# A transformer block on one core: the first two batches and the last one reordered

## The reference

```
h = gelu(x[1:] @ W1 + x[0] @ W2 + b)                      # 255 tokens
q, k, v = layernorm(h) @ qkv_w.T                           # 16 heads of 64
a = softmax(q k.T / 8 + bias[rel_bucket]) v                # per head
h = h + a @ o_w.T
h = h + (silu(layernorm(h) @ wg.T) * (layernorm(h) @ wu.T)) @ wd.T   # int weights / 127
```

## Time and profile before

| | us |
|---|---|
| median of 3 runs | 1799.73 (1798.41 to 1800.47) |
| profiled execution | 1802.05 |
| span of its instructions | 1799.9 |

### The profile page before, as it was taken

How to read it: one execution, slowest core, us unless ns; L and a number is a source line. 1 busy time by engine, 2 the same in 40 slices (tenths; PEclk the granted TensorE clock), 3 DMA queues, 4 the chain that set the end, 5 groups by cost and what they waited for, 6 DMA issues and landing times.

```text
span 1799.9 us, 47320 instructions
## 1 busy us (share of the span) xinstructions
PE 1765.0 (98%) x17460; PEld 1649.0 (92%) x17460; DVE 1517.0 (84%) x4832; ACT 1391.5 (77%) x3784; POOL 1165.3 (65%) x1493
## 2 busy tenths in 40 slices
PE   8899999999999999999999999999999999999997
PEld 6789999999999999999999999999999999999996
DVE  6788888988888988888988888888888888889885
ACT  6777778777787787877877778777787777877873
POOL 2666656766656766666766567666567666667663
PEclk9999999999999999999999999999999999999998
DMA  6200000000000000000000000000000000000000
GB/s 197 60 7 16 17 16 4 14 16 16 17 16 5 14 16 16 16 10 10 13 16 16 16 8 10 16 16 17 16 5 13 16 16 16 16 5 13 7 7 13
DMA packets 26777, 34.13 MB, mean 19 GB/s; under 512 B 3457, under 2 KB 20402, under 8 KB 26546
## 3 DMA queue, kind: packets, MB, share of 16 engines
q1 hardware_dynamic: 26368, 30.95, 5.8%
q10 hardware_dynamic: 178, 0.13, 0.0%
HBM read 22.65 MB, written 8.42 MB: 17 GB/s over the span
## 4 chain that ended last, share of the span: by engine, by line
PE 95%; DVE 2%; POOL 1%; ACT 1%; issue 1%; DMA 0%; POOLq 0%; DVEq 0%; ACTq 0%
PE ps L484 56%; PE ps L569 14%; PE ps L545 13%; PE ps L558 7%; PE ps L493 3%; PE ps L513 2%; DVE prob L992 1%; DVE pT L1000 0%; DMA staged<-w_v 0%; POOL prob L420 0%; PE ps L507 0%; ACT prob L802 0%; POOL wo L397 0%; DVE wg L923 0%; ACT xt L769 0%
## 5 line engine op out<-in xcount | busy, mean ns | idle before, releaser
L420 POOL TENSOR_TENSOR prob<-prob,inv 128x510 f32<-128x510 f32 x512 | 524.0, 1037 | 369.5 <-DVE inv L1005 369.5
L809 ACT ACTIVATE pT<-ps 128x512 fp32r<-128x512 f32 x512 | 278.3, 596 | 326.9 <-PE ps L558 326.9
L802 ACT ACTIVATE prob<-prob,neg_top 128x255 f32<-128x255 f32 x1024 | 506.9, 502 | 4.8 <-DVE neg_top L992 4.4
L992 DVE CUSTOM_DVE_ANT_0 prob<-ps,bias 128x255 f32<-128x255 f32 x1024 | 380.2, 420 | 98.9 <-PE ps L545 92.0
L484 PE MATMUL ps<-xnT,wqk 128*128 128x256 f32 x3072 | 414.6, 284 | 1.4 <-DVE qk L970 1.4
L484 PEld LDWEIGHTS ps<-xnT,wqk 128*128 128x128 f32 x3072 | 379.4, 188 | 13.8 <-DVE qk L970 1.6
L1000 DVE TENSOR_TENSOR pT<-ps,pT 128x512 fp32r<-128x512 f32 x512 | 334.6, 685 | 1.5 <-ACT pT L809 1.5
L569 PE MATMUL ps<-pT,v 128*128 128x256 f32 x2048 | 297.1, 288 | 20.2 <-DVE pT L1000 10.6
L569 PEld LDWEIGHTS ps<-pT,v 128*128 128x128 f32 x2048 | 265.8, 191 | 37.5 <-issue 30.8
L545 PE MATMUL ps<-qk 64*128 64x256 f32 x3072 | 252.4, 297 | 0.0
L545 PEld LDWEIGHTS ps<-qk 64*128 64x128 f32 x3072 | 198.8, 186 | 35.0 <-issue 0.8
(11 more groups left out here) (94 smaller groups left out, 2587.4 us busy)
## 6 DMA issues: line engine op xcount, KB each, us to landing
xt<-x_cols SPq DMA_DIRECT2D x32, 256.0 KB, 2.7
out<-xt SPq DMA_DIRECT2D x32, 128.0 KB, 1.7
r_rows<-readout_rows SPq DMA_DIRECT2D x30, 128.0 KB, 2.9
out<-xt SPq DMA_DIRECT2D x32, 112.0 KB, 1.9
bias<-bias_rows SPq DMA_DIRECT2D x8, 384.0 KB, 5.2
staged<-w_qk SPq DMA_DIRECT2D x8, 256.0 KB, 5.2
staged<-w_v SPq DMA_DIRECT2D x4, 256.0 KB, 5.8
staged<-w_o SPq DMA_DIRECT2D x4, 256.0 KB, 5.8
```

The costliest lines, as they stand in the source:

```text
L420: pool.tensor_tensor(pr, pr, by, ALU.mult).then_inc(prob_done, 1)
L802: ex = act.activation(pr, pr, ACT.Exp, bias=neg_top[:, g % 2, hh, t:t + 1], scale=-1.0, accum_out=total[:, g % 2, hh, t:t + 1])
L809: act.activation(transposed(0, half), transposed_in(half), ACT.Copy).then_inc(pT_hi, 1)
L992: ins = dve.tensor_tensor_reduce(prob[:, g % 2, hh, t, 0:S], ps[:, bank_s[hh], t * T:t * T + S], falling(2 * g + hh, WINDOW - 1 - b0), 1.0 ...
```

## The change

It reorders the written-out pipeline at three places. The computation is the same; the only new instructions are matmuls of `keep_busy`.

1. **First steps.** In step 0 DVE and ACT do the bias of the second head, both exponentials and both inverses of pair 0 before the low and high parts of weight pieces 6 to 9. Pieces are spread differently over steps 0 to 3 (10 and 11 stay in step 1, 12 and 13 in step 2, 14 to 16 in step 3), POOL's low part of piece 14 moves one step later. ACT does its pieces ahead of `heads_moved`, and DVE its pieces ahead of `heads_added` and of the first head's `add_bias` in all steps with pieces (0 to 10).
2. **Values of batch 0 and 1.** `values(0, 1)` goes behind the transposes of step 1, `values(0, 2)` from step 2 to step 4, `values(0, 3)` from step 4 to step 5 and into `bank_f`. `norm_transposed(0, 1)` writes `bank_f` and no longer waits for `probs_lo` of pair 4. ACT and DVE take `values(1, 1)` at the end of step 9, not in step 10 behind the probabilities. Five `keep_busy` matmuls stand ahead of the value product in steps 2 and 7, written into `bank_a`.
3. **The end.** In step 256 the transposes of the last pair come ahead of the projection; `down(30)` is cut in two halves of three tiles, one in step 256 and one in step 257; DVE takes its result (`output(30)`) ahead of the last `residual`; `keep_busy` has 9 and 3 matmuls around the value product of step 256 and 17 ahead of the last `norm_transposed`.

The core of the diff (in order: tables and banks, TensorE, ACT, DVE; the calls of `ln_bank` and `v_bank` get the batch, and the old place of ACT's pieces at the end of `step` is removed):

```diff
-        PIECES_AT = {0: (6, 7, 8), 1: (9, 10, 11), 2: (12, 13, 14), 3: (15, 16), 4: (17, 18),
+        PIECES_AT = {0: (6, 7, 8, 9), 1: (10, 11), 2: (12, 13), 3: (14, 15, 16), 4: (17, 18),
                      5: (19, 20), 6: (21, 22), 7: (23, 24), 8: (25,), 9: (26,)}
...
-        def ln_bank(n):
-            return (bank_t[1], bank_f)[n]
-
-        def v_bank(n):
-            return bank_s[0] if n == 3 else bank_f
+        def ln_bank(n, batch):
+            return bank_f if n == 1 or batch == 1 else bank_t[1]
+
+        def v_bank(n, batch):
+            return bank_s[0] if n == 3 and batch > 0 else bank_f
...
-                def keep_busy(n):
+                def keep_busy(n, bank=bank_qk):
                     for _ in range(n):
-                        pe.matmul(ps[:, bank_qk, 0:P], ident[:], ident[:], start=True, stop=True)
+                        pe.matmul(ps[:, bank, 0:P], ident[:], ident[:], start=True, stop=True)
 
...
-                def down(batch, has_lo):
-                    for m in range(MT):
+                def down(batch, has_lo, tiles=range(MT)):
+                    for m in tiles:
...
-                    mm.then_inc(dn_mm, 1)
+                    if m == MT - 1:
+                        mm.then_inc(dn_mm, 1)
...
-                            pe.wait_ge(v_lo, count(4, i, 0))
-                            values(i, 1)
-                        if g == 2 and i >= 2:
-                            if i < B:
-                                pe.wait_ge(biased, count(H, i, 2))
-                            else:
-                                pe.wait_ge(biased, count(H, B - 1, H - 1))
+                            if i > 0:
+                                pe.wait_ge(v_lo, count(4, i, 0))
+                                values(i, 1)
+                        if g == 2 and 2 <= i < B:
+                            pe.wait_ge(biased, count(H, i, 2))
                             down(i - 2, has_lo)
-                        if g == 4 and i < B:
+                        if G in (4, 5):
+                            pe.wait_ge(v_lo, count(4, 0, G - 3))
+                            values(0, G - 2)
+                        if g == 4 and 0 < i < B:
                             pe.wait_ge(biased, count(H, i, 6))
                             values(i, 3)
...
-                            pe.wait_ge(pT_lo, count(H, i, 8))
+                            if i > 0:
+                                pe.wait_ge(pT_lo, count(H, i, 8))
+                            else:
+                                pe.wait_ge(v_lo, count(4, 0, 3))
...
+                        if G == 1:
+                            pe.wait_ge(v_lo, count(4, 0, 0))
+                            values(0, 1)
+                        if g == 2 and 0 < i < B:
                             pe.wait_ge(v_lo, count(4, i, 1))
...
-                    if i < B:
-                        early()
+                    early()
+                    if G == PAIRS * B:
+                        keep_busy(9)
                     if pair(G - 2):
                         if pair(G - 3):
                             pe.wait_ge(o_added, count(PAIRS, *pair(G - 3)))
+                        if G in (2, 7):
+                            keep_busy(5, bank_a)
                         values_probs(*pair(G - 2))
+                    if G == PAIRS * B:
+                        keep_busy(3)
+                        transpose_banks_free()
+                        probs_transposed(*pair(G - 1))
                     if pair(G - 3):
                         bb, gg = pair(G - 3)
                         if gg == 0 and bb > 0:
                             pe.wait_ge(h1_done, count(1, bb - 1))
                         project(bb, gg)
-                    if i == B:
-                        early()
+                    if G == PAIRS * B:
+                        pe.wait_ge(biased, count(H, B - 1, H - 1))
+                        down(B - 2, has_lo, range(0, MT // 2))
+                    if G == PAIRS * B + 1:
+                        down(B - 2, has_lo, range(MT // 2, MT))
                     if pair(G):
                         score_banks_free()
                         scores(i, g)
                     if G == 0:
                         queries_keys(0, 1)
-                    if pair(G - 1):
+                    if pair(G - 1) and i < B:
                         transpose_banks_free()
                         probs_transposed(*pair(G - 1))
                     late()
 
                 def finish(has_lo):
+                    keep_busy(17)
                     norm_transposed(1, B - 1)
...
-                    if g == 2 and i < B:
+                    if g == 2 and i < B and i != 1:
                         values_hi(i, 1)
                     if g == 7 and prev:
                         tanh(i - 1, 4)
-                    if pair(G - 1):
+                    if pair(G - 1) and G > 1:
                         exps(*pair(G - 1), 0)
...
-                    if g == 4 and i < B:
+                    if g == 4 and 0 < i < B:
                         values_hi(i, 3)
+                    if G in (4, 5):
+                        values_hi(0, G - 2)
...
+                    if G == 0:
+                        exps(0, 0, 0)
+                        exps(0, 0, 1)
                     if g == 0 and 0 < i < B:
                         values_hi(i, 0)
+                    if g == 1 and i == 1:
+                        values_hi(i, 1)
...
+                    for n in PIECES_AT.get(G, ()):
+                        if n < FIRST_INT:
+                            piece_high(n)
...
-                    if g in (5, 7) and pair(G - 2):
+                    if i > 0 and g in (5, 7) and pair(G - 2):
                         probs_lo(*pair(G - 2), 1)
-                    if pair(G - 1):
+                    if pair(G - 1) and G > 1:
                         add_bias(*pair(G - 1), 1)
-                    if g not in (5, 7) and pair(G - 2):
+                    if (i == 0 or g not in (5, 7)) and pair(G - 2):
                         probs_lo(*pair(G - 2), 1)
                     if pair(G - 2):
                         probs_lo(*pair(G - 2), 0)
...
-                    if g == 2 and 2 <= i < B:
+                    if g == 2 and i >= 2:
                         output(i - 2)
...
+                    if G == 0:
+                        add_bias(0, 0, 1)
+                        inverse(0, 0, 0)
+                        inverse(0, 0, 1)
                     if g == 0 and 0 < i < B:
                         values_lo(i, 0)
+                    if g == 1 and i == 1:
+                        values_lo(i, 1)
...
                     if g == 3 and i == B:
-                        output(B - 2)
                         normalise(1, B - 1)
...
-                    if g != 1 and pair(G - 2):
-                        heads_added(*pair(G - 2))
-                    if pair(G) and G > 0:
-                        add_bias(i, g, 0)
                     for n in PIECES_AT.get(G, ()):
                         if n < FIRST_INT and n not in POOL_PIECES:
                             piece_low(n)
                     for n in PIECES_AT.get(G - 1, ()):
                         if n >= FIRST_INT:
                             piece_low(n)
+                    if g != 1 and pair(G - 2):
+                        heads_added(*pair(G - 2))
+                    if pair(G) and G > 0:
+                        add_bias(i, g, 0)
```

More of the change, by code:

```diff
@@ L512, in norm_transposed @@
                         for t in range(TT):
-                            mm = pe.transpose(ps[:, ln_bank(n), k * T + t * P:k * T + (t + 1) * P],
+                            mm = pe.transpose(ps[:, ln_bank(n, batch), k * T + t * P:k * T + (t + 1) * P],
                                               normed[:, t, k * P:(k + 1) * P], ident[:])
@@ L532, in values @@
                         pe.wait_ge(piece_lo, V_ALL if n else V_FIRST)
-                    split_mm(ps[:, v_bank(n), :], lambda a, k: xnT[:, a, k, t * P:(t + 1) * P],
+                    split_mm(ps[:, v_bank(n, batch), :], lambda a, k: xnT[:, a, k, t * P:(t + 1) * P],
                              lambda b, k: wv[:, b, k, half * 512:(half + 1) * 512], range(KD)
@@ L658, in score_banks_free @@
                             pe.wait_ge(out_done, count(1, i - 2))
-                        if g == 4:
+                        if g == 4 and i > 0:
                             pe.wait_ge(v_lo, count(4, i, 3))
@@ L783, in norm_hi @@
                     dst = (xnT, hnT)[n]
-                    act.activation(dst[:, 0].rearrange("p k n -> p (k n)"), ps[:, ln_bank(n), :], ACT.Copy
+                    act.activation(dst[:, 0].rearrange("p k n -> p (k n)"), ps[:, ln_bank(n, batch), :], ACT.Copy
                                    ).then_inc(lnT_hi[n], 1)
@@ L794, in values_hi @@
                     dst = v[:, t, half * 4:half * 4 + 4, :].rearrange("p g (s d) -> p g s d", d=DH)
```

(13 more changed lines are left out.)

6 lines of the change are left out of this document (3 added, 3 removed).

## The result

The changed kernel takes 1796.1 us (median of 18 runs, 1794.49 to 1797.29); the kernel before, on the same chip in the same session, 1800.2 us (18 runs, 1797.09 to 1803.17). The ratio is 0.9978, 95% interval 0.9971 to 0.9985: 0.22% faster, 4.1 us of the 8.1 forecast, at the edge of the range. The profiled execution of the changed kernel took 1795.17 us, 3.37 of them outside its span of 1791.8 us.

A forecast was written before the change was run, and what follows sets the result against it. PE was taken as full from 100 to 1763 us, so only its idle time and lowered clock at both ends could gain: head 3.6 plus end 4.5, 8.1 us off 1799.7, giving 1791.6 us; range 1788.5 to 1796.2.

The forecast's parts named there:

- First product, step 2: First value product: 0.69 us later, at 35.6, perhaps 0.86 shorter if idle matmuls hold the clock; together nothing.
- a late landing of piece 11: Step 2: weight piece 11 might land at 33.3 instead of the assumed 31.0, 2.3 us too late.
- Steps 3 to 5: Moved values groups of batch 0: POOL sets the pace, projection again at 56.6 to 56.7, gain 0 plus or minus 1.
- Steps 6 to 10: Later head: products at 61.2, 69.7 and 91.4; the head gains 3.6 us at full clock, 2.5 at half.
- steps 6 to 8: Transposes off the wait (0.69) and pieces filling DVE's waits (1.3): product of pair 4 gains 2.0 us.
- The end: From 1763.7 us: last transposes at 1780.0, not 1784.49, gain 4.5 us; 17 idle matmuls overrun by 0.35.
- (c): Rival, chance 0.04: idle matmuls do not hold the clock at the end; slower, 1804.0 us.
- (a): Rival, chance 0.22: the end gains, but DVE pieces held up by POOL cost the head's 3.6 us; 1795.2 us.
- (b): Rival, chance 0.13: POOL gets ahead in steps 3 to 5, step 10's gap shrinks below 2 us; 1788.5 us.
- (d): Rival, chance 0.08: waits move to other engines at both ends, 1.5 us in each; 1797 us.
- Sum: Whole kernel: head 3.6 plus end 4.5 gives 8.1 us, taken from the median 1799.7 to 1791.6.
- its two cases: Step 10, gap of 2.4 us: head gains 3.6 us with the full clock, 2.5 with the half; called even.

The follow-up runs named there:

- the two dead-branch edits: The change with only its untaken branch edited: 29 idle matmuls of the end left out there (1795.86 us, 0.997), or one added there (1796.55 us, 0.9971).
- end only: Only the end changed, first steps ordered as in the kernel before: 1797.45 us, ratio 0.9974 to the kernel before, span 1795.3.
- the parts alone: The change's first ten steps with the old end: 1799.07 us, 0.9987; its end with the old first steps: 1797.45 us, 0.9974.

## Why the prediction was half right

**First product, step 2.** Forecast 35.6. It came at 34.51 with the zero mark 0.91 earlier, so at 35.4 on the scale of before, and took 1.21 us: the full clock, in this execution. In those of the two dead-branch edits, whose running code is the same, the product took 2.07 and 1.95 us behind gaps of 2.11 and 2.04, so five idle matmuls make it likelier, not sure: over all profiles, the product had the full clock in five of seven with five idle matmuls ahead of it, and in one of five with none. The step's worry, a late landing of piece 11, did not come true: ACT began on it at 29.92 (30.8 on the scale of before; the forecast took 31.0).

**Steps 3 to 5.** Right: the projection waits for POOL again, at 55.87, or 56.8 on the scale of before (forecast 56.6 to 56.7). But this gain of 0 is counted from an execution of the kernel before whose first product had the half clock; with the full one, in end only, the old order has this projection at 55.1.

**Steps 6 to 10.** On the scale of before the products stand at 62.2, 69.8 and 92.6, forecast 61.2, 69.7 and 91.4; the gap of step 10 was 2.66 (2.4). The one after it is at 99.5 (98.4). At step 11 the head had gained 3.0 us (forecast 102.56 - 98.4 = 4.1), at the next product 2.9 (forecast 3.6).

The term that failed here is the 2.0 us of steps 6 to 8, which the working gave to the order: the transposes taken off the wait, and weight pieces that fill DVE's waits. The product of pair 4 came 1.0 earlier, not 2.0. DVE's waits for scores and for `heads_moved` did shrink, from 9.6 to 2.4 us between 20 and 100 us, but the product did not come earlier for it: the old order with the full clock in step 2 has this product 1.45 us ahead of before, 0.4 more than the changed kernel. So most of the head's gain was the clock behind the first product and in step 10, and some 0.2 us of it was order.

**The end.** Forecast 4.5, measured 4.6 in this pair, and 4.3 in the medians of end only. Of the working only the overrun was wrong: the 17 idle matmuls ended with `normalise`, not 0.35 after it.

**Rivals.** (c) falls: after nine idle matmuls the product took 1.19. (a) happened in small. In the changed kernel a piece met a pair of normalised heads:

```profile
34.60 2.04 POOL L420 TENSOR_TENSOR prob<-prob,inv 128x510 f32<-128x510 f32 x2 [7.98 <-DVE inv L1031]
```

```profile
35.90 1.29 DVE L949 TENSOR_TENSOR wo<-staged,wo 128x512 fp32r<-128x512 f32 x1
```

It took 1.29 where 0.68 is usual, with 0.74 us of POOL's work left at its start. The Trainium skill, "SBUF — State Buffer", section "Who interferes with whom", would let it wait for all of these 0.74; the 0.6 measured comes near. But DVE's low parts of pieces from 20 to 100 us add up to 14.8 us, against 14.0 before, so such meetings cost 0.8 us more than before and not up to 4, since others went away. The median lies near (a)'s 1795.2 all the same, by another way. (b) falls: at the projection POOL was no earlier, and the gap of step 10 stayed at 2.66. (d) falls at the end, where the wait for POOL went from 1.77 to 0.82 us. In the head it was in part right: from 20 to 100 us DVE's wait for the exponentials, ahead of `inverse`, grew from 2.7 to 4.5 us.

**Sum: the step that failed.** It took 3.6 + 4.5 us from one profiled execution and carried them to the median unchanged ("with the same distance the forecast is 1799.7 - 8.1"). But most of both terms was the price of gaps that ended in the half clock in that execution, and this is drawn anew in each. The profiled execution lay 2.3 us above the median; the working named this and did not ask what it consisted of. An execution with more of its gaps at the half clock has more to gain, so these 2.3 us were part of the 8.1, and were subtracted a second time. The 8.1 us between the two profiled spans split up so: 1.85 by which the first lay above its kernel's median span (1799.9, and 1800.2 - 2.15 = 1798.05), 0.75 by which the other lay below its own (1791.8 and 1792.55), and 5.5 of real gain in the span. Of these 5.5, 1.2 went outside the span, which only this program has at 3.4 and not at 2.1 us: 4.3, beside the 4.1 of the medians. So the sum left out two things: the draw (2.6) and the time outside (1.2).

The split takes the difference of the medians as the real gain; it is an account and not a test. The working saw the draw in one place, step 10, called it even, and then put the whole of the favourable case into the forecast; half of the 1.1 us between its two cases would have been the fair term by its own odds, and the full clock came there in one profile of six. It took the gaps of 2.51 and 2.10 us at the end of the kernel before as sure losses of the clock, where the second profile shows both products at the full clock and the fall only behind them. In the medians of the parts alone the end is near its term (4.3 of 4.5), the head is not (2.7 of 3.6), and the two together (5.2) are less than their sum. Whether that is more than the uncertainty of three ratios is not settled, nor whether the draw in one gap hangs on another. The idle matmuls alone point the same way: 4.0 us of span with those of the end, 4.75 with those of the head besides, in two sessions.

What the change gains is clock, by its 39 idle matmuls: without them 0.9997, with 49 in the old order 0.9969. The new order of the softmax, the transposes and `down`, in which the forecast put most of its working, is worth some 0.2 us in the head (at most 0.7) and 0.4 at the end, each read from one pair of profiles; the medians show nothing of it.

## What to carry to other kernels

Before costing a gap on TensorE by what followed it in one profile, look at the granted clock of several executions of the same kernel: here the span of one kernel went with its clock over some 3 us, most of the whole gain. Compare an order with another only where both held the clock, and look past the first instruction behind a gap. Where TensorE waits ahead of matmuls and nothing depends on it in the wait (the waits filled here were 0.9 to 3.5 us long), short idle matmuls into a free bank, with the order left alone, gave as much as the idle matmuls and the reordering together. Compare medians, and look at the time outside the span when an edit is worth about a microsecond.

## What the runs showed of the hardware

**One gap, two outcomes.** A gap of 2.51 us at the end of the kernel before ended in the half clock in one execution and in the full clock in another, at the same place behind the same work; so did one of 2.66 or 2.67 us in step 10 of the change. Behind gaps of 3.39 and 3.07 the product had the full clock once; behind a gap of 1.79 the clock fell once. The fall can also come later: behind a gap of 2.75 us the product took 1.18 us, and only the scores after it 1.65 in place of 0.98. Short idle matmuls in the gaps take this away almost wholly: the mean clock of the runs was 0.9996 with the most of them, and 0.993 with none. The Trainium skill, "TensorE: Matmul & The Clock Gate", section "What's actually happening", says that the gate follows how busy the engine has been recently. The traces agree in the direction, but none of the gaps named here could have been called from its length.

**A microsecond outside the span.** 3.1 to 3.4 us in three samples of one program and 2.1 in all the others, one of which differs from it by a single instruction that never runs.
